# Partial products of the query/key pairs and the out-projection: summed in PSUM and copied by ScalarE into gate-weight columns

## What is computed

```python
qkv = x @ w_qkv.T                      # 4096 x 512 times 512 x 1536
q = q * cos + _rotate_half(q) * sin    # the same for k
keep = (rel >= 0) & (rel < window)     # window is 64
attn = jax.nn.softmax(where(keep, q k^T * scale, -inf))
out = (attn @ v) @ w_out.T
x = _layernorm(x + out)
gate = jax.nn.silu((x @ w_gate) * s_gate)
up = (x @ w_up) * s_up
x = _layernorm(x + ((gate * up) @ w_down) * s_down)
```

## Time and profile before

| what | us |
|---|---|
| median of 3 runs (lowest, highest) | 1166.68 (1166.36, 1168.07) |
| span of the profiled execution, first to last instruction | 1164.2 |
| PE busy | 1154.0 |
| DVE busy | 984.6 |
| ACT busy | 584.4 |
| POOL busy | 587.3 |

### The profile page before, as it was taken

The page is one execution under the profiler, slowest core; times in us unless marked ns, Lnnn a source line. Parts: engine busy times, 40 slices in busy tenths (PEclk is TensorE's granted clock), DMA queues, the critical chain, the costliest instruction groups (busy, mean ns, idle before and its releaser), DMA issues.

```text
span 1164.2 us, 25539 instructions
## 1 busy us (share of the span) xinstructions
PE 1154.0 (99%) x8433; PEld 567.9 (49%) x8433; DVE 984.6 (85%) x2821; ACT 584.4 (50%) x1640; POOL 587.3 (50%) x563
## 2 busy tenths in 40 slices
PE   9999999999999999999999999999999999999998
PEld 4344446444464444644455444554445444464444
DVE  7899998898987899879998899897898988986434
ACT  3953883048820588105880169701686027950330
POOL 0775684156731667326771367613676236752330
PEclk9999999999999999999999999999999999999999
DMA  9999786366562765617656096561964537734000
GB/s 295 173 175 252 137 166 160 66 88 137 111 149 55 110 131 107 145 41 128 132 97 141 37 146 119 101 132 46 155 123 88 131 63 137 120 73 109 19 2 36
DMA packets 352077, 134.80 MB, mean 116 GB/s; under 512 B 309840, under 2 KB 332496, under 8 KB 351952
## 3 DMA queue, kind: packets, MB, share of 16 engines
q1 hardware_dynamic: 334976, 106.86, 49.6%
q0 software_dynamic: 10560, 17.30, 5.1%
q10 hardware_dynamic: 6416, 9.00, 2.1%
HBM read 32.19 MB, written 8.39 MB: 35 GB/s over the span
## 4 chain that ended last, share of the span: by engine, by line
PE 97%; DVE 1%; ACT 1%; issue 1%; POOL 0%; POOLq 0%; DVEq 0%
PE bank L842 61%; PE bank L1058 18%; PE bank L848 10%; PE bank L984 3%; PE bank L964 2%; PE bank L864 1%; PE bank L1080 1%; ACT bank L1243 1%; PE bank L873 0%; PE bank L1069 0%; PE bank L948 0%; DVE wd L1373 0%; ACT wu L1186 0%; DVE ffn_tmp L1530 0%; ACT fuse L1186 0%
## 5 line engine op out<-in xcount | busy, mean ns | idle before, releaser
L842 PE MATMUL bank<-x1T,wg 128*128 128x512 f16 (+1 forms) x1032 | 242.5, 378 | 0.0
L842 PE MATMUL bank<-x1T,wu 128*128 128x512 f16 x1024 | 241.9, 379 | 0.0
L1243 ACT ACTIVATE bank<-bank,neg_max,qk_scale 128x128 f32<-128x128 f32 x512 | 220.5, 435 | 7.8 <-DVE neg_max L1558 6.1
L1058 PE MATMUL bank<-wd,fuse 128*128 128x512 f16 (+2 forms) x1056 | 222.7, 373 | 0.0
L660 POOL TENSOR_TENSOR fuse<-ffn_tmp,fuse 128x512 f16<-128x512 f32 x128 | 149.7, 1170 | 117.5 <-ACT fuse L1186 116.8
L742 POOL TENSOR_TENSOR fuse<-fuse 128x512 f16<-128x512 f32 x116 | 137.7, 1218 | 74.9 <-ACT fuse L1186 72.8
L1058 PEld LDWEIGHTS bank<-wd,fuse 128*128 128x128 f16 x1056 | 101.9, 98 | 118.0
L842 PEld LDWEIGHTS bank<-x1T,wu 128*128 128x128 f16 x1024 | 100.1, 98 | 120.7
L655 POOL TENSOR_TENSOR xT_sb<-probs,xT_sb 128x512 f16<-128x512 f32 x112 | 129.6, 1158 | 44.5 <-ACT xT_sb L1186 44.4
L842 PEld LDWEIGHTS bank<-x1T,wg 128*128 128x128 f16 x1032 | 96.3, 98 | 113.9 <-issue 4.0
L1196 ACT ACTIVATE ffn_tmp<-bank,tanh_scale 128x512 f32<-128x512 f32 x128 | 88.2, 689 | 100.0 <-PE bank L842 76.8
(11 more groups left out here) (235 smaller groups left out, 1621.5 us busy)
## 6 DMA issues: line engine op xcount, KB each, us to landing
v_cross<-v_own SPq DMA_DIRECT2D x64, 128.0 KB, 2.4
out<-x ACTq DMA_DIRECT2D x31, 256.0 KB, 2.0
xT_sb<-xT SPq DMA_DIRECT2D x30, 256.0 KB, 4.1
qkT<-x SPq DMA_DIRECT2D x28, 256.0 KB, 3.8
wg<-w_gate POOLq DMA_DIRECT2D x7, 1024.0 KB, 5.2
wu<-w_up POOLq DMA_DIRECT2D x7, 512.0 KB, 6.0
wqkv<-w_qkvT SPq DMA_DIRECT2D x8, 256.0 KB, 6.3
wg<-w_gate POOLq DMA_DIRECT2D x1, 2048.0 KB, 8.4
```

What stands on the lines that cost most here:

```text
L842: last = pe.matmul(dst, lhsT, rhs, start=(i == 0), stop=(i == len(pairs) - 1))
L1058: last = pe.matmul(dst[:, cols], fuse[:, s, z, rows], wd[:, s, cols], start=(s == 0 and z == 0), stop=(s == STEPS - 1 and z == 1))
L1243: last = act.activation(unit, unit, ACT.Exp, bias=neg_max[:, s % 2, h // 3, h % 3:h % 3 + 1], scale=qk_scale[:, 2:3], accum_out=row_sum[:, ...
```

## The change

Products are added to each other in PSUM by PE itself: a matmul that does not start its bank anew adds to what is there. Between two products of such a chain ACT copies the running sum out, because the intermediate value is also needed.

- Query/key pair: the order is now first, fifth, sixth, second, seventh, third, fourth. First, sixth, seventh and fourth all go into bank `pair_banks(i)[2]`, fifth and third into `[1]`. ACT makes four copies of 128 x 512 (`keep_first`, `keep_fifth`, `keep_sixth`, `keep_seventh`), counted by `products_kept`, and PE waits for them. DVE does three additions (`add_front_even`, `add_back_odd`, `add_front_odd`).
- Out-projection pair: the order is first, seventh, sixth, fourth, fifth, third, second, in two banks (2i and 2i + 1). ACT makes four copies of 256 columns, counted by `o_products_kept`. DVE does four updates of 512 columns (`add_outer_kept`, `add_inner_kept`, `add_inner`, `add_outer`), and then `proj_added` waits for the last of them and raises `proj_read`.
- The copies go to columns 1024 to 2047 of `wg` ("late" columns, used from step 8), except for pair 0 of the query/key products, which uses `rope_other` in `fuse`. So both `wg` and `wu` are loaded up to column 1023 in `first()`, and in step 2 of every turn POOL issues the load of the late columns of both (`reload_late_columns`); PE waits for it at step 8.
- In `first()` the second product of the pair now stands between the last two groups of weighted values, the first one ahead of the last out-projection of tile 0, and `project_v(1, 0)` behind the pair. POOL also makes the operand sums of pair 0 there (`sum_first_x(0)`), which no product of that tile uses; the counts of `x_summed` are eight per tile from the start.

```diff
+            def pair_sixth(a, i):
+                wait(products_kept, pe, a - 1, 4 * turn_of(i))
+                done(sixth_product, quarter(pair_banks(i)[2], x_sums(i)[:, 1, :, :], w_sums[:, 0, :, :], True))
...
+                wait(x_summed, pe, a - 1, 7)
+                pair_fifth(a, i)
+                pair_sixth(a, i)
+                pair_second(a, i)
+                pair_seventh(a, i)
+                pair_third(a, i)
+                pair_fourth(a, i)
...
                     if s == 14:
-                        project_v(a + 1, 0, True)
-                project_pair(a + 1, 1, True)
+                        for j in range(2, NB):
+                            wait_xT(pe, a + 1, j)
+                        wait(proj_read, pe, a, 1)
+                        pair_second(a + 1, 1)
+                wait(proj_read, pe, a, 2)
+                pair_first(a + 1, 1)
+                project_o(a, NB - 1, ffn)
...
+                pair_fifth(a + 1, 1)
+                pair_sixth(a + 1, 1)
+                pair_third(a + 1, 1)
+                pair_seventh(a + 1, 1)
+                pair_fourth(a + 1, 1)
+                project_v(a + 1, 0, True)
...
+            def proj_added(a, i):
+                wait(o_summed, dve, a - 1, 4 * i + 3)
+                dve.sem_inc(proj_read[0], 2)
...
+                if s == 2:
+                    reload_late_columns(a, f, attn)
...
                 split_high(a + 1, 0, True)
+                keep_first(a + 1, 1)
                 for j in range(2):
                     split_x1_high(a, j, ffn)
                 split_high(a + 1, 1, True)
-                keep_first(a + 1, 1)
+                keep_fifth(a + 1, 1)
+                keep_sixth(a + 1, 1)
+                keep_seventh(a + 1, 1)
                 carry_v(a + 1)
...
                 if more:
+                    keep_seventh(a + 1, 0)
                     keep_first(a + 1, 1)
                     split_high(a + 1, 0, ffn)
+                    keep_fifth(a + 1, 1)
+                    keep_sixth(a + 1, 1)
+                    split_high(a + 1, 1, ffn)
+                    keep_seventh(a + 1, 1)
                     carry_v(a + 1)
-                    split_high(a + 1, 1, ffn)
```

More of the change, by code:

```diff
@@ L351, in build @@
         HALF_EMB = EMB // 2
+        LATE = INTER // 2
         SWAPPED = 4 * P
@@ L839, in _, with product, quarter @@
         def _(pe):
-            def product(dst, pairs):
+            def product(dst, pairs, onto=False):
                 for i, (lhsT, rhs) in enumerate(pairs):
-                    last = pe.matmul(dst, lhsT, rhs, start=(i == 0), stop=(i == len(pairs) - 1))
-                return last
+                    last = pe.matmul(dst, lhsT, rhs, start=(i == 0 and not onto), stop=(i == len(pairs) - 1),
+                                     skip_group_check=onto)
+                return last
+            def quarter(dst, lhsT, rhs, onto=False):
+                return product(dst, [(lhsT[:, k, :], rhs[:, k, :]) for k in range(KC // 2)], onto)
             def qkv(j, part, dst, parts=range(KC)):
@@ L878, in project_odd, with pair_first @@
                     done(qk_done, last)
-            def project_pair(a, i, first=False):
-                front_even, front_odd, back_even, back_odd = pair_banks(i)
+            def pair_first(a, i):
                 front_low, front_high, back_low, back_high = x_quarters(i)
                 low_even, odd_less_even, high_even, high_odd = w_quarters()
-                sums, turn = x_sums(i), turn_of(i)
-                def quarter(dst, lhsT, rhs):
-                    return product(dst, [(lhsT[:, k, :], rhs[:, k, :]) for k in range(KC // 2)])
+                done(first_product, quarter(pair_banks(i)[2], front_low, low_even))
@@ L906, in project_pair @@
[L906 to L913 removed]
+                wait(*((proj_read, pe, a - 1, NB - 1) if i == 0 else (down_read, pe, a - 2, NB - 1)))
@@ L1001, in project_o_pair @@
             def project_o_pair(a, i):
-                front_left, front_right, back_left, back_right = o_places(i)
+                second, chain, third, other = o_places(i)
                 front_low, front_high, back_low, back_high = o_quarters(i)
@@ L1144, in body @@
                         wait(columns_in, pe, f - 1, 31)
+                    if s == STEPS // 2:
+                        wait(late_columns_in, pe, f, 31)
                     if s >= 2:
@@ L1331, in body @@
                         keep_first(a + 1, 0)
+                    if more and j == 3:
+                        keep_fifth(a + 1, 0)
+                        keep_sixth(a + 1, 0)
                     wait(y_ready, act, f, j)
@@ new lines, in add_outer, with add_inner @@
+            def add_outer(a, i):
+                wait(proj_done, dve, a, 2 * i + 1)
+                wait(o_summed, dve, a - 1, 4 * i)
+                done(o_summed, add_to_rows(outer_rows(i), in_halves(bank32[2 * i])))
+            def add_inner(a, i):
+                wait(o_product, dve, a - 1, 6 * i + O_THIRD)
+                wait(o_summed, dve, a - 1, 4 * i + 1)
+                done(o_summed, add_to_rows(inner_rows(i), bank32[2 * i + 1]))
+            def proj_added(a, i):
+                wait(o_summed, dve, a - 1, 4 * i + 3)
+                dve.sem_inc(proj_read[0], 2)
@@ L1837, in front @@
                     add_back_o(a, 0)
-                    add_back_right(a, 0)
-                    add_front_left(a, 0)
-                    sum_o_second(a, 0)
-                    sum_o_third(a, 0)
-                    sum_o_fourth(a, 0)
-                    add_back(a, 0)
-                    add_back_left(a, 0)
-                    add_front(a, 0)
-                    add_front_right(a, 0)
+                    add_outer_kept(a, 0)
+                    add_inner_kept(a, 0)
+                    add_inner(a, 0)
+                    add_outer(a, 0)
+                    proj_added(a, 0)
                     keep_o(a, STEPS // 2 - 1)
```

303 lines of the change are left out of this document (123 added, 180 removed).

## The result

The changed kernel takes 1182.3 us (median of four runs, 1177.6 to 1183.1), the kernel before 1166.5 us beside it. The ratio is 1.0123, 95% interval 1.0101 to 1.0145: slower, as forecast, but by more than twice the 7.0 us forecast and 2.3 us above the upper end of the range. The profiled execution took 1183.1 us, with a span of 1181.3 us against 1164.2 before.

The account below looks back on a forecast made before the run. PE, busy 99%, was taken to bound the kernel, so time freed on DVE gains nothing. Out-projection 3.9 plus end of `first()` 3.1 gave 7.0 us more: span 1171.2, median 1173.7 us, range for 8 in 10 1168.0 to 1180.0.

Parts of the forecast that it names:

- the late loads: Reloading late columns each turn, 2 MB more: hidden before step 8, price 0, up to 1 us a turn.
- Two microseconds are left: Steps 2 and 3 of a turn: spare time of the transposes beside the loads, after POOL's issues delay them by 0.5.
- (d): End of `first()`: `split_x1(2)` behind ACT's last copy and `carry_v` moves to about 109.3; price 0, at most 1 us.
- Just in time: End of `first()`: DVE ends block 3's rope products at 119.3, PE wants the scores at 119.7; price 0.
- Query/key pairs of the turns: Twelve pairs where PE waits for ACT's copies: 0.5 to 0.9 us left everywhere, price 0, at most 7 us.
- ACT is the new bound: Rival, chance 0.15: ACT's copies come late in the turns' query/key pairs and PE waits; 1179.7 us.
- Out-projection: Pairs of the turns: pair 1's third product waits for `add_back_o(2)`, 0.55 us late, seven times, 3.9 us; bounds 0 and 5.6.
- (a): End of `first()`: the pair's first product waits for `take_x1(2)` ahead of block 3's out-projection, at least 0.5 us.
- (b): End of `first()`: POOL's four more additions slow DVE ahead of `take_x1(2)`, 0 to 2.9 us more, taken as 1.5.
- (c): End of `first()`, order third, seventh, fourth: fourth product waits 0.9 us for ACT's copy, third 0 to 0.5, taken as 0.2.
- The bound of 8 us: Upper price of the late columns' loads over all turns, up to 1 us a turn if the queue is worse.
- the loads delay the transposes: Rival, chance 0.05: the late columns' loads hold up the transposes for steps 2 and 3; 8 us more, 1181.7 us.

Follow-up runs that it names:

- `take_x1(2)` early: Changed kernel with `take_x1(2)` moved on DVE in `first()` between `finish_x1(0)` and `finish_x1(1)`, ahead of `rope_sums`: 1180.7 us, ratio 1.0120.
- ACT's new order: Changed kernel with ACT's `split_x1_high(2)` and `(3)` ahead of `keep_seventh` and `carry_v` at the end of `first()`: 1178.7 us, ratio 1.0095.

## Why the prediction was wrong in size

The direction was right, and so were the places where waits were forecast. Three steps failed: the late loads, priced at 0 because "Two microseconds are left", cost 4.2 us; part (d) of the end of `first()`, priced at 0 as "Just in time", cost 1.8; and the wait for `take_x1(2)`, 0.5 + 1.5 us, was counted at its length alone and cost 4.5, of which 1.7 us are products at 1.2 GHz.

- **Query/key pairs of the turns, 0.** Right: 24.03 to 24.10 us for 56 matmuls. The rival "ACT is the new bound" falls.
- **Out-projection, 3.9 us.** Right in place, cause and size: 7 x 0.56 us by the trace, and moving `keep_o(7)` took 3.7 us of it away.
- **(a) and (b), the wait for `take_x1(2)`: forecast 0.5 + 1.5, measured 4.5.** The 1.5 us that POOL's additions cost DVE came out: two times 0.53 for `rope_sums` and 0.4 for the second `finish_x1`. But 1.5 was half of a range, so this was in part luck, and the reading that it rested on was off. The two `finish_x1` of 3.27 us are not 1.6 each; the first takes 2.81 and the second 0.54:

```profile
87.70 2.81 DVE L1600 TENSOR_SCALAR x<-x,mean_var,rstd 128x512 f32<-128x512 f32 x1
```

  The long one ends 0.29 us behind `sum_w(3)` (90.51 against 90.22), and in the changed kernel 0.34 us behind it (92.42 against 92.08). The rule of the Trainium skill (SBUF — State Buffer, "SBUF: two separate sides") would have given 2.2, so the rows lie between none and a full lock of each instruction. What failed is the step behind it: I took a wait of PE at its length. In the rows it comes with a fall of the clock to 1.2 GHz, which cost 1.7 us more. The other 0.8 us is that PE was there 1.0 us later than I reckoned (93.44 and not 92.4), but DVE 1.9 us later beside POOL's 1.5, because `sum_w(3)` started at 89.73 and not at 87.86. In the second profile of the changed kernel it started at 88.89, and the wait was 2.2.
- **(c), 0.9 + 0.2.** The fourth product's wait is as reckoned (0.85). The third's 0.2 is not there in the changed kernel, as PE was late itself; it is 0.75 where PE was not (`take_x1(2)` early).
- **(d), forecast 0, at most 1, measured 1.8.** The failed step is "Just in time". I let `split_x1(2)` move to about 109.3 and DVE gain 2 us from there to the end of the rope products of block 3. It moved to 112.47, since PE was later, and DVE gained 0.7 (12.05 us before, 11.36 now), so the rope products ended at 123.83 and not at 119.3; the first group of scores started at 123.15 and not near 119.7, and the second waited 0.38 us. And I followed one consumer, the scores, where DVE's queue feeds more: `split_v` stands behind the same rope products, gate 0 waits for its blocks 0 and 1 and gate 1 for block 3, and these two waits are 1.3 of the 1.8 us. ACT's new order took all of it away.
- **Late columns, forecast 0, at most 1 a turn, measured 4.2 by the trace and 4.3 in the kernel before with the loads alone.** The failed step is the sentence "Two microseconds are left". It used 3 to 5 us for the transposes, which is what they take alone, while the loads run beside them on the same 16 DMA engines. In turn 3 the first was issued 0.4 us late, as forecast, and landed 5.0 us later after its issue than before; before, it had landed 5.1 us ahead of its first use. The second landed 3.5 us later, with 2.8 us to spare. The Trainium skill (DMA: Bandwidth & Descriptors, "Queues, rings and completion order") says that each DMA engine goes round its queues packet by packet; the rows agree in so far as both sides slow down: the transposes as said, and the load of 1 MB of w_gate, 5.0 to 5.3 us in the turns of the kernel before, takes 6.4 to 7.8 in turns 1 to 6. The bound of 8 us in the text held, but I gave it a chance of 0.05.
- Of the rivals, "the loads delay the transposes" had the right mechanism and half its price. The forecasts on DVE and ACT's busy time were 60 and 39 us; measured 41 and 35.

The sum of what was measured in the terms forecast to cost (3.95 + 4.5 + 0.85) is 9.3 us, against 7.0; the two terms forecast at nothing add 6.0. That makes 15.3 of the 17.1 us of the profiled execution.

## What to carry to other kernels

When one engine is 99% busy, price what a change moves before what it saves: here the cost came from 3.4 us of products that no longer stood in front of a wait, from the order of two queues, and from loads that pay for a place to park the sums. Ask of a DMA that is added beside others what they have to spare, reckoned with more than their time alone: here it went to 2.1 and 2.6 times. And count a stall of TensorE for both, its length and what the products behind it take if the granted clock falls.

## What the runs showed of the hardware

- The clock fell with a single wait in an otherwise full stretch. In these profiles the granted clock of 96 to 100 us was 1.00 where PE's wait there was 0.8, 1.77 or 1.84 us, and 0.50 to 0.71 where it was 2.0 to 4.65 us. Two profiled executions whose waits differ by 0.2 us (1.84 and 2.02) thus differ by 1.6 us more. This may be part of the changed kernel's spread of 1177.6 to 1184.5. Of its eight executions the three with a mean granted clock of 0.999 took 1177.6 to 1180.2 us and the five with 0.997 or 0.998 took 1181.9 to 1184.5, which fits; but the clock also falls at the very end of a run, and only two of the eight were profiled, so it isn't shown.
- DVE and POOL lengthen each other: 0.68 to 1.21 us for a two-input addition on DVE, 0.72 to between 0.90 and 1.16 for one on POOL.
- Two loads of 1024 KB and two transposes in flight together: in turn 3 the transposes landed 8.05 and 6.76 us after their issue instead of 3.06 and 3.29; with one load beside them it was 5.37 and 4.02 us, and nobody waited.
- Matmuls that add onto a bank which ACT has just read take as long as those that start one: 24.0 us for the fourteen quarter products in both kernels.
